# Edge scores of a graph attention layer: POOL waits for each slot of eight gathers before it goes on

## What is computed

```python
xl = (x @ Wl + bl).reshape(n_nodes, H, C)
xr = (x @ Wr + br).reshape(n_nodes, H, C)
e = jax.nn.leaky_relu(xl[src] + xr[dst], NEG_SLOPE)
alpha = jnp.einsum('ehc,hc->eh', e, att)
m = jax.ops.segment_max(alpha, dst, num_segments=n_nodes)
```

## Time and profile before

| | us |
|---|---|
| median of 3 runs | 7766.42 |
| lowest, highest | 7758.99, 7787.47 |
| span of the profiled execution | 7865.6 |
| edge scores of layer 1, first gather to last reduce | 4106.3 to 5452.0 |
| edge scores of layer 2 | 5980.9 to 7329.2 |

### The profile page before, as it was taken

One profiled execution on the slowest core, in us unless ns is written; L12 is line 12 of the kernel. 1 busy time (PEld: TensorE's weight loads), 2 busy tenths in 40 slices (PEclk: granted clock), 3 DMA queues, 4 the chain that ended last, 5 costly groups with the idle time before them and its releaser, 6 DMA issues. The chain is left out here.

```text
span 7865.6 us, 104440 instructions
## 1 busy us (share of the span) xinstructions
PE 4297.8 (55%) x26852; PEld 3458.2 (44%) x26923; DVE 4772.7 (61%) x7334; ACT 2362.7 (30%) x3661; POOL 3733.3 (47%) x4217
## 2 busy tenths in 40 slices
PE   5777777310279545555535444444695444444397
PEld 2677776310179545555523222222683222222396
DVE  4666666688521156566547666666665766666675
ACT  5444444117322145555522111111222111111121
POOL 3666566100200166666625555553654555655363
PEclk9555555555589777777767666666896766666696
DMA  8677777895578533233225656564654666656462
GB/s 313 191 219 212 222 203 226 228 236 191 215 250 307 183 112 115 96 117 114 91 72 147 159 152 156 154 157 119 135 134 114 157 158 155 160 150 158 100 140 75
DMA packets 1472089, 1296.30 MB, mean 165 GB/s; under 512 B 1257993, under 2 KB 1297567, under 8 KB 1459038
## 3 DMA queue, kind: packets, MB, share of 16 engines
q1 hardware_dynamic: 902378, 671.59, 28.5%
q0 software_dynamic: 167008, 441.69, 21.0%
q10 hardware_dynamic: 402580, 181.62, 8.4%
HBM read 942.23 MB, written 351.27 MB: 164 GB/s over the span
## 5 line engine op out<-in xcount | busy, mean ns | idle before, releaser
L2503 POOL DMA_INDIRECT rows_p<-node_rows,stage_i x1632 | 1546.5, 948 | 1228.0 <-issue 978.9
L2557 PE MATMUL psZ<-parts_r,hot_t 128*128 x4896 | 1164.3, 402 | 1360.5 <-DVE lz L2638 867.7
L2557 PEld LDWEIGHTS psZ<-parts_r,hot_t 128*128 128x128 bf16 x4896 | 590.0, 121 | 1938.6 <-issue 1624.4
L2646 DVE TENSOR_TENSOR psZ<-psZ,rows_p 128x1320 f32<-128x1320 f32 x408 | 626.5, 1536 | 768.9 <-remote 283.0
L731 POOL DMA_INDIRECT rows_s<-hpx,hpST x784 | 741.4, 946 | 486.4 <-issue 203.8
L1961 POOL DMA_INDIRECT both<-table,srcI x784 | 741.9, 946 | 431.5 <-issue 211.1
L749 PE MATMUL psP<-window,pair_hot 128*128 x3136 | 701.9, 416 | 249.0 <-ACT pair_hot L771 146.6
L749 PEld LDWEIGHTS psP<-window,pair_hot 128*128 128x128 f32 x3136 | 672.8, 325 | 279.2 <-issue 279.0
L828 DVE SCALAR_TENSOR_TENSOR pair_run<-pair_run,same_c,psP 128x64 f32<-128x64 f32 x1568 | 440.2, 281 | 469.1 <-PE psP L749 209.1
L2953 PE MATMUL ps_steps<-A,xs 128*65 128x125 f32 x5184 | 578.8, 272 | 137.8 <-DVE A L2971 93.1
L2638 DVE SCALAR_TENSOR_TENSOR lz<-psZ,att 128x1320 f32<-128x1320 f32 (+2 forms) x428 | 642.6, 1501 | 8.4
(11 more groups left out here) (545 smaller groups left out, 7260.0 us busy)
## 6 DMA issues: line engine op xcount, KB each, us to landing
tile<-adj SPq DMA_DIRECT2D x168, 781.2 KB, 4.9
xs<-x_src SPq DMA_DIRECT2D x432, 128.0 KB
x_src<-rows_p SPq DMA_DIRECT2D x204, 256.0 KB
hpx<-stage ACTq DMA_DIRECT2D x25, 2048.0 KB
window<-hpx SPq DMA_DIRECT2D x196, 256.0 KB
dst_runs<-pair_run SPq DMA_DIRECT2D x28, 1792.0 KB
eaT<-in_ea SPq DMA_DIRECT2D x28, 1792.0 KB
adj<-tile SPq DMA_DIRECT2D x42, 781.2 KB
```

The costliest lines, as they stand in the source:

```text
L2503: pool.indirect_dma_start(rows[:, k, j, :], None, g.node_rows, bass.IndirectOffsetOnAxis(stage[:, k, j:j + 1], 0)).then_inc(got[k], 16)
L2557: last = pe.matmul(psZ[:, n % 2, j, 0:ZH], hot[:, k, col * CE:(col + 1) * CE], parts[:, bass.ds(at[col], 1), q, :].rearrange("p o c -> p ( ...
L2646: v.tensor_tensor(here, here, rows[:, slot, at * G:(at + 1) * G, 0:ZH], ALU.add).then_inc(added, 1)
```

## The change

One line is added at the end of the loop over the slots, behind the eight gathers. POOL now waits until all gathers of the slot that it has just issued have landed, and only then looks at the next slot. The count is the one for which SP and DVE wait already.

```diff
@@ -2502,6 +2502,7 @@
                         for j in range(KS):
                             pool.indirect_dma_start(rows[:, k, j, :], None, g.node_rows,
                                                     bass.IndirectOffsetOnAxis(stage[:, k, j:j + 1], 0)).then_inc(got[k], 16)
+                        pool.wait_ge(got[k], i * (16 * KS) + 16 * KS)
 
             @block.tensor
             def _(pe):
```

## The result

| us | before | after |
|---|---|---|
| first comparison, median of 6 runs each | 7776.89 | 7812.84 |
| lowest, highest | 7758.99, 7793.37 | 7807.17, 7826.52 |
| span of the profiled execution | 7865.6 | 7814.1 |
| edge scores of layer 1, first gather to last reduce | 1345.7 | 1338.4 |
| edge scores of layer 2 | 1348.2 | 1338.9 |

The traces say the opposite sign (the span falls by 51 us), because the profiled execution of before lay 89 us above its median and that of after 3 us above its own. Only 16.6 us of those 51 lie in the two stages; 32.5 lie ahead of layer 1's first gather (4106.3 against 4073.8), in code that the change doesn't touch.

The account below looks back on a forecast made before the run. No engine was full; a ring of waits bound it, DVE's slot release pacing POOL and PE pacing DVE. Median 7766.42, -2 us for the edge-score stages and +6 for profiled against ordinary runs gave 7770 us, range 7685 to 7860.

Parts of the forecast that it names:

- The pause: POOL's stop behind each slot's eight gathers: landing 2.46 plus restart 0.85, 3.31 us where 0.30 stood.
- The "faster" rival (2.76): POOL resumes 0.30 us after landing, so it stops 2.76 us behind a slot; 7655 us in all; chance 0.18.
- The turn: Three slots of the edge-score loop at POOL's pace, 12.99 us each: 38.97 us.
- The crawl goes: PE and SP, slow while SP's DMAs meet running gathers, mostly recover; the remainder, 4.5 to 9 us a turn, is hidden.
- SP's DMAs meet gathers at every slot: Slower rival: three meetings a turn, each some 4.5 us for PE; +136 us, 7900; chance 0.17.
- The slot release by DVE sets POOL's pace, and PE sets DVE's: Edge-score loop before the change: POOL waited 5.63 us for DVE's add, which had waited 4.94 us for PE.
- nearly the same length: In the edge-score turns DVE's release wait, some 11 us of DVE idle, goes; POOL's own pace limits instead.
- Turn 0 stays as it is: Each stage's first turn: its three slots end by 4145, before DVE's first add at 4152.54, so no time changes.
- 1295.6 forecast: Turn 1 to last reduce of each edge-score stage: 98 slots 1273.0, eight gathers 9.7, landing 2.5, DVE's tail 10.4 us.
- -2: Both edge-score stages from turn 1 to last reduce: +1.7 us in layer 1 and -3.8 in layer 2.
- +6 us: Whole kernel: allowance for time given back being a bit smaller in an ordinary run than in a profiled one.
- the profile flatters the change: Slower rival: the profiler lengthens the kernel before, ordinary turns are 37.3 us, so 60 to 90 us lost; 7840; chance 0.13.

Follow-up runs that it names:

- even steps: One, two and three landing waits a turn added to the kernel before, where it took 6812 to 6821 us: +188, +380 and +576 us.
- short condition: Comparisons in which the unchanged kernel before took 6812.46 to 6821.47 us; turn 30.04 us, no slow PE or SP instructions.
- long condition: Comparisons in which the unchanged kernel before took 7776.89 to 7874.52 us, with slow PE and SP instructions; turn 38.61 us in its first trace.
- the second trace: The changed kernel run again, unchanged, on a fifth chip: 7839.47 against 7851.57 us for the kernel before (0.9987).
- the trace with one wait: Kernel before plus a landing wait behind slot 1 only, once a turn, where before took 7831.28 us: 7855.58 us (1.0028).

## Why the prediction was right, and where not

**The pause: right.** 3.31 us forecast, 3.15 measured as the mean of turns 5 to 32, about 3.0 behind slots 0 and 1 and 3.42 before the loop's branch. Its parts: landing 2.41 for 2.46, restart 0.70 for 0.85 in the row above. The "faster" rival (2.76) fell: a semaphore's release costs POOL more than going on from one gather to the next, as the even steps of the short condition confirm. By the Trainium skill ("DMA: Bandwidth & Descriptors", section "Anatomy of one DMA — SWDGE (gpsimd) path") the pause was estimated at 2.36; the lowest mean behind a waited slot in any trace is 2.97.

**The turn: right, and to the hundredth by luck.** 38.97 forecast, 38.97 and 38.87 in the long condition, 38.93 in the short one. It is POOL's own arithmetic, so it does not care about the condition. But the three pauses came out 0.47 us a turn shorter than forecast, and the 21 gaps inside slots longer by as much: 0.323 us on average, not 0.30. Nearly all of them are 0.305; 12 times in 58 turns (5 to 33, both layers) the gap between a slot's first and second gather was 2.0 us, for which the sum had no term.

**The crawl goes: right, but not for the reason given.** Slow instructions fall from 506 to none (1 in the second trace). The rival "SP's DMAs meet gathers at every slot" fell. The set's last two DMAs do overlap the first gather of the next slot (4254.24 to 4254.95 in the row above), and no crawl starts. The prediction tied the crawl to SP's DMAs meeting running gathers and called that a coincidence without a known cause; the trace with one wait shows that it begins without them, late in a long stretch of gathers. By that reading it goes because no stretch outlasts eight gathers. No run varied the length of the stretch with SP's DMAs held in their places, so this is argued, not shown.

**What paced the kernel before: half right.** "The slot release by DVE sets POOL's pace, and PE sets DVE's" holds for the long condition only. I took from one turn that POOL passes from slot 1 to slot 2 without a pause; over the stage the pause behind slot 1 is 2.92 us, near the other two. The crawl moves from slot to slot and costs a turn some 8.3 us of pauses (9.24 less 0.94), whichever slot it hits. The forecast of "nearly the same length" was right because the waits cost 8.5 (9.46 less 0.94); the nearness of these two numbers is all there is to the result.

**Turn 0 stays as it is: wrong.** It became 12.9 us shorter (51.76 to 38.85), and the first add came 25.3 us after the first gather, not 46.2: PE's and DVE's first work crawled as well, since POOL issued 24 gathers in a stretch there: PE's pairs of products at L2531, 0.8 us apart until 4117.20, then come up to 5.7 us apart until 4139.76 (PE's weight loads in the trace of before, with SP's first DMA at 4118.35):

```profile
4116.38 0.30 PEld L2531 LDWEIGHTS psZ<-wB,hT 128*128 128x128 f32 x2 [0.52 <-DVE parts_r L2632]
4117.20 0.30 PEld L2531 LDWEIGHTS psZ<-wB,hT 128*128 128x128 f32 x2 [0.52 <-DVE parts_r L2632]
4119.20 0.30 PEld L2531 LDWEIGHTS psZ<-wB,hT 128*128 128x128 f32 x2 [1.70 <-issue]
4124.88 0.50 PEld L2531 LDWEIGHTS psZ<-wB,hT 128*128 128x128 f32 x2 [5.39 <-DVE parts_r L2632]
```

The step that failed is "its three slots end before DVE's first add", which took DVE's start as given. In layer 2 turn 0 went from 48.8 to 39.0 us. From turn 1 to the last reduce the stages took 1299.5 and 1300.0 us, 4 us more than the 1295.6 forecast. So -2, +8.3 and -22.7 make the -16.6 us that the two stages gained in the traces (7.3 + 9.3).

**The sum against the median: the term that was mis-sized.** I put +6 us for the difference of profiled and timed runs. Measured, the stages gave 17 us back in the traces, and yet the runs became 36 us longer. The rival "the profile flatters the change" (7840) describes the sign, but not with its reason, a profiler that lengthens the crawl: in the long condition later on, the profiled executions lay within 13 us of their medians (before 7868.69 for 7874.52, changed 7826.94 for 7839.47). Rather the first profiled execution of before, at 7866, seems to belong to a part of the spread that its timed runs didn't show: medians of before were 7777, 7831, 7852 and 7875 in four comparisons, those of the changed kernel 7813 and 7839 in two. Against 7777 the change costs 0.45%, against 7852 it costs nothing. There is no trace of before at 7777. If the rest of the program was then as long as in the trace of after (7814.1 less 2677.3), its two stages together took about 2640 us, some 19 us a stage less than the changed kernel's. That is an estimate, and it wasn't shown: the rest of the program was itself 5136.8 to 5171.7 us long in the seven long traces, though no run changes it.

**The price that the first profile couldn't show.** In the short condition the same change costs 8.4%. All its rows were those of the long condition; nothing in them says that another exists. Had the comparison met the short one, 7397 us would have lain far outside the range of 7685 to 7860: that it met the long one is luck.

**Slips in the prediction's sums.** They move no verdict. The faster rival's 7655 leaves out the +6 that the forecast has; with it, it is 7661. In the rival on the profile the turn of before by its own working, (1293.9 - 10.4) / 33, is 38.9 and not 38.7, and a turn of 37.3 against 38.97 would cost 110 us over 66 turns, not 60 to 90.

**Open.** What sets the condition: chips 961 us apart run the same program, and one chip had both. What slows PE and SP late in a long stretch of gathers in the long condition, and why landing ends it: the store's size is ruled out, and it starts without SP's DMAs too, but no run left them out, or varied the stretch alone. In the short condition 24 gathers without a pause do no harm. Why before varies by 98 us within the long condition.

## What to carry to other kernels

A wait for one's own DMA costs its landing and a restart, here 2.8 us beyond the usual 0.30, and it is free only while another chain is at least as late; so ask how firm that other chain is, since it may be the trouble of one condition of the machine. Idle time of equal length before and after is no sign that nothing happened: look at the releasers. Where a profiled execution lies 1% off its median, take a second trace before resting a sign on it. A version fit for both conditions would remove the crawl without pausing POOL; none was found here. A coincidence seen in one kernel (SP's DMAs and the crawl) can come apart in a variant of it, so look for the order of events there before naming a trigger.

## What the hardware showed that was not expected

- The same program took 6812 to 6821 us in three comparisons and 7777 to 7875 in four, at equal durations of one gather (945 to 948 ns). One and the same chip gave both.
- In the long condition small register and MOVE instructions of PE and SP take mostly 0.7 us and up to 1.6 us each, where 0.03 to 0.05 us is usual, from some 9 us after the start of a stretch of gathers without a pause until the gathers have landed. With the wait behind slot 1, this began in 42 of 65 such stretches before SP's first DMA amid them. Cutting SP's store from 256 to 32 KB didn't remove it (622 slow instructions, 506 and 469 with the full store). With a pause behind every eight gathers it is gone (0 and 1).
- Pausing POOL behind one slot of three didn't shorten the others' crawl: the pauses of a turn stayed 9.2 us in sum.
- Between a slot's first and second gather POOL paused 2.0 us instead of 0.305 12 times in 58 turns of the changed kernel, and never in the kernel before in the short condition. What causes it is open.
